# Decoder of two layers on one core: output of the second cross attention added later, two heads rounded at once, sixteen buffers for gathered rows

## Chip, core and metric

The kernel runs on one core of one Trainium2 chip. The metric is the device time of one execution in microseconds; the time before is the median of three runs.

## What is computed

Eight sequences of 256 tokens of width 256 (2048 tokens in all, 16 tiles of 128) go through two decoder layers. Each layer adds to x, one after the other, the results of an attention, a cross attention to a context of 64 tokens and a mixture of experts, each on the layer-normalised x. The part that changes most is the cross attention of the second layer, where the context of all eight sequences counts as one of 512 tokens and queries, keys, values and weights are rounded to whole steps:

```python
q = (x @ Wq + bq).reshape(1, B * N, H, hd)          # 16 heads of 16
kv = (cond @ Wkv + bkv).reshape(1, -1, 2, H, hd)
q, k = _fq_sym(q * scale, axis=-1), _fq_sym(k, axis=-1)
v = _fq_sym(v, axis=2)                               # one step per value column
attn = softmax(einsum('bhqd,bhkd->bhqk', q, k))
attn = _fq_unsigned(attn, axis=-1)                   # round(x / s) * s, s = max / 255
out = einsum('bhqk,bhkd->bhqd', attn, v)
return out @ Wp + bp
# experts of layer 1: 4 of 16 per token, and a shared expert
out = shared / (k + 1) + moe_out * (k / (k + 1))
```

## The kernel before

The five engines run five programs written out ahead, in the order attention, cross attention, experts of layer 0, then the same of layer 1. Each instruction raises a counter, and `at(name, ...)` names the value that another waits for; a queue waits in order, so whatever stands behind a waiting instruction waits with it. SP issues the plain DMAs, POOL (GpSimd) the gathers and scatters by index.

**Second cross attention (class `Cross1`).** The loop runs over 16 steps (h) for each of 16 tiles (t), one score of a head in each step, plus three tiles' worth of steps to drain. Every engine has the same loop with its own lag. In step i PE makes the score of unit i (L1608, one of three PSUM banks, each free after its exponential), the transposes of the rounded weights of unit i-6 (L1618), and every second step the product with the values (L1630). DVE makes the maximum of unit i-1 (L1704) and the rounding of unit i-3 (L1709, five buffers in, five out). POOL makes from the maximum a bias of one column (L1798). ACT makes the exponential of unit i-1 with this bias (L1765) and every second step copies the transposed weights of two heads out of PSUM (L1772). Around these, at fixed h, stand the steps of the tile: the output product of tile t-2 (`pe_o`, h=0) and its addition to x (L1729, h=1), the query product of tile t+1 (`pe_q`, h=2), the seven DVE steps that scale and round the queries (`dve_queries`, one each step from h=3), their build on POOL (L1793, h=9), the transpose (L1602, h=11) and the copy on ACT (L1760, h=12). The output of tile t-1 is normalised at h=9, transposed at h=12 and multiplied at h=13 by the value scales `sv` (L1741, two instructions). POOL adds the output bias to x at h=10 (L1813). In odd tiles DVE and POOL also make the layer norms of two tiles for the experts and two for the next queries (L242 to L257, L250); from the fourth tile on the routing (L1160 to L1194) runs beside the steps, and POOL issues eight scatters to `xs_scratch` (L1381), one every second step from h=14 of an even tile on.

**Experts (class `Experts`).** After the slots of the experts, each token's rows (2 in layer 0, 4 in layer 1) are gathered from `ys_scratch` by POOL (`fetch`, L1406), one DMA for 128 rows, and DVE adds each with its gate to x (`add`, L1326). There are 8 buffers in either layer, and a gather waits for the add that last used its buffer. In layer 1 the shared expert runs in the same stretch for tiles 4 to 15 (products L219, ACT L1371, DVE L1312 and, into x, L1317); DVE's order is two of its steps, then one tile's adds. In layer 0 the adds stand at the head of the attention of layer 1, interleaved with it. SP stores a tile of x after its last add.

## Time and profile before

| | us |
|---|---|
| median of three runs | 1522.99 |
| lowest and highest | 1522.81, 1527.49 |
| profiled execution, its own time | 1528.68 |
| its span | 1526.9 |
| busy: PE, DVE, ACT, POOL | 1214.9, 886.4, 679.5, 429.2 |

The profile is that of one execution. Its rows give the start and the length of an instruction or of several merged, the engine, the line, what is written and read, and in brackets how long the engine had been idle before it and what ended that. Lengths of neighbours overlap a little, since an instruction begins before the one ahead has written all. Starts are counted from the start of the span.

### The profile page before, as it was taken

Reading aid. Unit: us, or ns where it says so; the run is one execution under the profiler, and the core shown is the slowest. Engines: PE = TensorE matmul, PEld = TensorE weight load, DVE = VectorE, ACT = ScalarE, POOL = GpSimd, SP = SyncE. Lnnn points to the kernel's source line nnn. Section 1 sums busy time; section 2 is a strip of 40 time slices with the busy share of each in tenths; the row PEclk is TensorE's granted clock in tenths of the full one; section 3 lists DMA queues with packets and bytes.
Section 4 is the critical chain, followed back from the end, with each engine's and each line's share of the span. In section 5 each row is a group of like instructions: output and inputs, shape, how many; then the busy total and the mean of one; then the engine's idle time right before and its main releaser. Section 6 shows DMA issues by size and latency. Waiting matters only on the chain.

```text
span 1526.9 us, 25789 instructions
## 1 busy us (share of the span) xinstructions
PE 1214.9 (80%) x8208; PEld 848.6 (56%) x8255; DVE 886.4 (58%) x2522; ACT 679.5 (45%) x1412; POOL 429.2 (28%) x682
## 2 busy tenths in 40 slices
PE   5799989982999998478887676777777649999982
PEld 3467766771566665346565354555555435777641
DVE  4546654762232222467676699898888842644354
ACT  2334544320211111134444699989889832333110
POOL 1001101447000000423422243554555441000365
PEclk8799999995999999579898788778787759999997
DMA  7756644012111111543521200000000013454333
GB/s 165 154 118 141 145 107 166 28 42 86 38 44 47 46 45 49 150 103 91 140 58 25 111 2 1 29 22 19 18 29 29 22 49 108 149 155 154 114 103 110
DMA packets 83200, 122.59 MB, mean 80 GB/s; under 512 B 13639, under 2 KB 71111, under 8 KB 79568
## 3 DMA queue, kind: packets, MB, share of 16 engines
q1 hardware_dynamic: 73852, 95.78, 23.5%
q0 software_dynamic: 9216, 25.18, 5.4%
q8 instruction: 69, 1.13, 0.3%
q14 instruction: 63, 0.51, 0.1%
HBM read 76.73 MB, written 43.78 MB: 79 GB/s over the span
## 4 chain that ended last, share of the span: by engine, by line
PE 46%; issue 19%; DVE 11%; POOL 7%; DMA 7%; ACT 6%; SPq 2%; another core or an unknown queue 2%; POOLq 0%; DVEq 0%; ACTq 0%
PE ps L219 13%; PE ps L1070 13%; PE ps L1087 6%; POOL work L1798 3%; DMA W<-q_parts 3%; ACT work L1765 2%; PE ps L423 2%; PE ps L1055 2%; POOL xs_scratch L1381 2%; PE ps L1079 2%; PE ps L443 2%; DVE work L559 1%; PE ps L458 1%; PE ps L426 1%
## 5 line engine op out<-in xcount | busy, mean ns | idle before, releaser
L1070 PE MATMUL ps<-W,work 128*128 x628 | 225.5, 492 | 3.9 <-issue 3.9
L1765 ACT ACTIVATE work<-ps,work 128x512 f32<-128x512 f32 x256 | 204.6, 812 | 31.1 <-POOL work L1798 30.6
L1295 DVE TENSOR_TENSOR work<-work,ps 128x128 f32<-128x128 f32 (+1 forms) x118 | 49.7, 421 | 238.5 <-ACT work L1361 238.5
L1704 DVE TENSOR_REDUCE work<-ps 128x1 f32<-128x512 f32 x256 | 173.3, 677 | 14.3 <-remote 6.9
L559 DVE TENSOR_REDUCE work<-ps 128x2 f32<-128x512 f32 (+1 forms) x192 | 128.3, 685 | 89.8 <-PE ps L426 87.8
L1608 PE MATMUL ps<-SM,work 128*128 128x512 bf16 x209 | 100.9, 485 | 93.4 <-ACT work L1765 91.6
L662 ACT ACTIVATE work<-ps 128x512 f32<-128x512 f32 x192 | 112.9, 601 | 112.8 <-PE ps L446 105.3
L1070 PEld LDWEIGHTS ps<-W,work 128*128 128x128 f32 x628 | 110.9, 191 | 69.0 <-issue 64.7
L1798 POOL TENSOR_SCALAR work<-work 128x1 f32<-128x1 f32 x256 | 93.4, 365 | 176.4 <-DVE work L1704 166.4
L1772 ACT COPY work<-ps 128x1024 bf16<-128x1024 bf16 x128 | 132.1, 1032 | 8.2 <-PE ps L1618 8.1
L250 POOL TENSOR_TENSOR rstd<-ve,half 128x1 f32<-128x1 f32 x96 | 54.3, 571 | 276.7 <-DVE ve L246 274.3
L1618 PE MATMUL ps<-idb,work 128*128 128x128 bf16 x1024 | 122.2, 255 | 6.2 <-ACT work L1765 3.2
L1087 PE MATMUL ps<-W,work 128*128 x470 | 121.0, 380 | 0.0
L1361 ACT ACTIVATE work<-ps 128x128 f32<-128x128 f32 (+1 forms) x118 | 45.4, 384 | 164.2 <-PE ps L1070 164.1
L1406 POOL DMA_INDIRECT W<-ys_scratch,work x64 | 62.8, 982 | 192.6 <-DMA ys_scratch<-work 162.9
L423 PE MATMUL ps<-W 102*128 102x256 bf16 (+3 forms) x512 | 84.3, 273 | 39.1 <-DMA W<-q_parts 19.3
L1709 DVE TENSOR_SCALAR work<-work 128x512 bf16<-128x512 f32 x256 | 108.3, 423 | 11.2 <-ACT work L1765 9.8
L1618 PEld LDWEIGHTS ps<-idb,work 128*128 128x128 bf16 x1024 | 87.6, 115 | 32.5 <-issue 20.7
L1608 PEld LDWEIGHTS ps<-SM,work 128*128 128x128 bf16 x256 | 28.2, 110 | 131.5 <-ACT work L1765 116.6
L219 PE MATMUL ps<-xnT,W 128*128 128x512 f32 (+1 forms) x224 | 90.4, 559 | 6.7 <-ACT work L1371 3.9
L1357 ACT COPY work<-ps 128x256 f32<-128x256 f32 x118 | 44.1, 374 | 97.0 <-PE ps L1055 97.0
L1087 PEld LDWEIGHTS ps<-W,work 128*128 128x128 f32 x470 | 80.2, 190 | 12.1 <-issue 0.4
(246 smaller groups left out, 2366.3 us busy)
## 6 DMA issues: line engine op xcount, KB each, us to landing
work<-xs_scratch SPq DMA_DIRECT2D x118, 128.0 KB, 2.1
ys_scratch<-work SPq DMA_DIRECT2D x118, 128.0 KB, 1.9
q_parts<-work SPq DMA_DIRECT2D x48, 128.0 KB
W<-k_parts SPq DMA_DIRECT2D x48, 128.0 KB
W<-q_parts SPq DMA_DIRECT2D x16, 384.0 KB
W<-in_w_in SPq DMA_DIRECT2D x6, 1024.0 KB, 11.1
W<-q_parts SPq DMA_DIRECT2D x16, 256.0 KB
W<-in_w_out SPq DMA_DIRECT2D x1, 4096.0 KB, 20.0
```

Source lines behind the costliest of these rows:

```text
L219: mm = q.e.matmul(out_, l, r, start=start and i == 0, stop=i == n - 1, skip_group_check=True)
L423: q.e.matmul(PS[bk][:, w * i:w * i + w], qs[0:NA, h, 128 * j:128 * j + 128], ks[0:NA, h // self.per, 0:w], start=i == 0, stop=False, skip_ ...
L559: q.e.tensor_reduce(self.m[:, j, h0:h0 + n], ov, AX, ALU.max).then_inc(*up("mx", L, b, u))
L662: q.e.activation(self.pt(b, g, kind), PS[banks.of["ps2", L, b, g, kind]][:, :], ACT.Exp, scale=0.25).then_inc(*up("exp", L, b, g, kind))
L1070: mm = q.e.matmul(PS[bks[c]][:, 0:N], self.XT[s % 2][:, k, :], w[:, k, bass.ds(regs[s] + 512 * c if c else regs[s], N)], start=k == 0, sto ...
L1087: mm = q.e.matmul(PS[bk][:, 0:256], self.UT[s % 2][:, 128 * c:128 * c + 128], w[:, bass.ds(regs[s] + 256 * c if c else regs[s], 256)], sta ...
L1608: q.e.matmul(PS[bk][:, :], self.q3T[t % 2][:, h // 2, :], kM[:, h, :], start=True, stop=True).then_inc(*up("c1_s", t, h))
L1618: mm = q.e.transpose(PB[bk][:, 512 * (h % 2) + 128 * c:512 * (h % 2) + 128 * c + 128], self.ei[(H * t + h) % 5][:, 128 * c:128 * c + 128], ...
L1704: q.e.tensor_reduce(self.mm[:, h:h + 1], PS[banks.of["c1_s", t, h]][:, :], AX, ALU.max).then_inc(*up("c1_mx", t, h))
L1765: q.e.activation(self.ee[n % 5], PS[banks.of["c1_s", t, h]][:, :], ACT.Exp, bias=self.nb[:, h:h + 1], scale=self.sq[t % 2][:, h:h + 1], ac ...
L1772: q.e.copy(self.aT[n % 3], PB[banks.of["c1_at", n]]).then_inc(*up("c1_aT", n))
L1798: q.e.tensor_scalar(self.nb[:, h:h + 1], self.mm[:, h:h + 1], self.nsq[t % 2][:, h:h + 1], LN255, ALU.mult, ALU.add).then_inc(*up("c1_nb", ...
```

## The change

In the second cross attention, the output is added to x at h=3 instead of h=1, and the queries' steps begin at h=4 instead of 3; their build on POOL moves from h=9 to 10, their transpose from 11 to 12, their copy on ACT from 12 to 13; the output's transpose moves from 12 to 11 and the addition of the output bias from 10 to 11. One instruction rounds the weights of two heads, in even steps, with three buffers of two heads in and two out. The value scales are multiplied into the output weights once, by two instructions at the start of DVE's part, and the transposed output is copied by one instruction. In the experts the adds of a tile wait for all of its gathers, the gathers of a tile for the adds of the tile four before, and layer 1 has 16 buffers.

```diff
-                    self.YG = [xall[1][:, i, :] for i in range(8)]
+                    self.YG = [xall[1][:, i, :] for i in range(16)]
...
             def add(self, q, t):
                 L, K = self.L, self.K
+                q.wait_ge(at(f"g{t % 4}", L, t, K - 1), at("x_b0", t) if L == 0 else at("x_s", t))
                 for j in range(K):
-                    i = (K * t + j) % 8
-                    q.wait_ge(at(f"g{i}", L, t, j), at("x_b0", t) if L == 0 else at("x_s", t), q.chain(), at("x_e", L, t, j - 1))
-                    q.e.scalar_tensor_tensor(out=x[:, t, :], in0=self.YG[i], scalar=self.gk[:, t, j:j + 1], in1=x[:, t, :],
+                    q.wait_ge(q.chain(), at("x_e", L, t, j - 1))
+                    q.e.scalar_tensor_tensor(out=x[:, t, :], in0=self.YG[(K * t + j) % len(self.YG)], scalar=self.gk[:, t, j:j + 1],
...
             def fetch(self, q, t):
+                q.wait_ge(at("x_e", L, t - 4, K - 1))
                 for j in range(K):
-                    i = (K * t + j) % 8
-                    n = K * t + j - 8
-                    q.wait_ge(at("x_e", L, n // K, n % K))
...
-                self.ee = [wk(512) for _ in range(5)]
-                self.ei = [wk(256, BF) for _ in range(5)]
+                self.ee = [wk(1024) for _ in range(3)]
+                self.ei = [wk(512, BF) for _ in range(2)]
...
-                    if h == 11 and t + 1 < T:
+                    if h == 12 and t + 1 < T:
                         self.pe_qt(q, t + 1)
-                    if h == 12 and 1 <= t < T + 1:
+                    if h == 11 and 1 <= t < T + 1:
                         self.pe_ot(q, t - 1)
...
             def dve_round(self, q, t, h):
-                n = H * t + h
-                q.wait_ge(at("c1_exp", t, h), at("c1_at", *self.unit(n - 5)))
-                q.e.tensor_scalar(self.ei[n % 5], self.ee[n % 5], MAGIC, MAGIC, ALU.add, ALU.subtract).then_inc(*up("c1_ei", t, h))
+                n = 8 * t + h // 2
+                q.wait_ge(at("c1_exp", t, h), at("c1_at", *self.unit(2 * n - 3)))
+                q.e.tensor_scalar(self.ei[n % 2], self.ee[n % 3], MAGIC, MAGIC, ALU.add, ALU.subtract).then_inc(*up("c1_ei", n))
...
+                q.wait_ge(at("kv_Vq"), at("w_cr1", "bp"))
+                for k in range(2):
+                    e.tensor_scalar(wp1[:, k, :], wp1[:, k, :], sv[:, k:k + 1], None, ALU.mult).then_inc(*up("c1_wp", k))
...
-                    if 3 <= i < self.N + 3:
+                    if 3 <= i < self.N + 3 and i % 2 == 0:
                         self.dve_round(q, *self.unit(i - 3))
-                    if h == 1 and 2 <= t < T + 2:
+                    if h == 3 and 2 <= t < T + 2:
                         q.wait_ge(at("c1_o", t - 2), at("c1_xb", t - 2))
...
-                    if h == 3 and t + 1 < T:
+                    if h == 4 and t + 1 < T:
                         queries.append(self.dve_queries(q, t + 1))
...
-                        for k in range(2):
-                            m = e.tensor_scalar(self.OnT[:, k, :], PS[banks.of["c1_ot", t - 1]][:, 128 * k:128 * k + 128], sv[:, k:k + 1], None, ALU.mult)
-                            m.then_inc(*(up("c1_OnT", t - 1) if k else q.step()))
+                        e.tensor_copy(self.OnT, halves(PS[banks.of["c1_ot", t - 1]][:, 0:256])).then_inc(*up("c1_OnT", t - 1))
...
-                q.wait_ge(at("c1_nb", t, h), at("c1_ei", *self.unit(n - 5)), at("c1_rs", t - 2))
+                q.wait_ge(at("c1_nb", t, h), at("c1_ei", n // 2 - 3), at("c1_rs", t - 2))
...
-                    if h == 12 and t + 1 < T:
+                    if h == 13 and t + 1 < T:
                         self.act_q3T(q, t + 1)
...
-                    if h == 9 and t + 1 < T:
+                    if h == 10 and t + 1 < T:
                         self.pool_Q3(q, t + 1)
-                    if h == 10 and t < T:
+                    if h == 11 and t < T:
```

## Rows read from the trace of the kernel before

**Rows 1.** Busy time of each engine in the stretch, granted clock, DMA share.
```profile
857.00:1235.00 378.00, 269.02 (x2637) 193.59 (x2681) 331.84 (x918) 340.40 (x675) 182.88 (x361) 0.78 0.06 22
```
**Rows 2.** Groups by form, 857 to 1235: busy us, mean ns, idle before, releasers.
```profile
L1765 ACT ACTIVATE work<-ps,work 128x512 f32<-128x512 f32 x256 | 204.6, 812 | 31.1 <-POOL work L1798 30.6
...
L1704 DVE TENSOR_REDUCE work<-ps 128x1 f32<-128x512 f32 x255 | 172.7, 677 | 10.5 <-PE ps L1608 5.8 <-remote 3.1
L1709 DVE TENSOR_SCALAR work<-work 128x512 bf16<-128x512 f32 x256 | 108.3, 423 | 11.2 <-ACT work L1765 9.8
...
L1729 DVE TENSOR_TENSOR x<-x,ps 128x256 f32<-128x256 f32 x15 | 6.3, 421 | 17.1 <-PE ps L219 17.1
```
**Rows 3.** The exponential's line (L1765): whom it waited for (us, times).
```profile
  POOL work L1798: 30.6, 52
```
**Rows 4.** Tail, POOL: group of the gathers from 1425.7 us, columns as in rows 2.
```profile
L1406 POOL DMA_INDIRECT W<-ys_scratch,work x64 | 62.8, 982 | 192.6 <-DMA ys_scratch<-work 162.9 <-issue 15.2 <-DVE x L1326 14.5
```
**Rows 5.** Tail, POOL in order of time: the first and the last of the 64 gathers.
```profile
1428.74 0.98 POOL L1406 DMA_INDIRECT W<-ys_scratch,work  x1 [162.86 <-DMA ys_scratch<-work]
...
1520.39 0.95 POOL L1406 DMA_INDIRECT W<-ys_scratch,work  x1 [0.30 <-issue]
```
**Rows 6.** Tail, DVE in order of time.
```profile
1451.46 0.42 DVE L1317 SCALAR_TENSOR_TENSOR x<-ps,x 128x256 f32<-128x256 f32 x1 [7.98 <-remote]
...
1505.07 0.42 DVE L1317 SCALAR_TENSOR_TENSOR x<-ps,x 128x256 f32<-128x256 f32 x1 [3.15 <-remote]
1505.41 4.82 DVE L1326 SCALAR_TENSOR_TENSOR x<-W,work,x 128x256 f32<-128x256 f32 x9
...
1523.14 0.48 DVE L1326 SCALAR_TENSOR_TENSOR x<-W,work,x 128x256 f32<-128x256 f32 x1 [0.61 <-DMA W<-ys_scratch,work]
```
**Rows 7.** Order of time, start of an even tile.
```profile
1038.44 2.02 PE L219 MATMUL ps<-W,work 128*128 128x256 f32 x4
...
1040.25 0.63 PE L1608 MATMUL ps<-SM,work 128*128 128x512 bf16 x1
...
1040.50 0.42 DVE L1729 TENSOR_TENSOR x<-x,ps 128x256 f32<-128x256 f32 x1 [1.43 <-PE ps L219]
...
1040.83 0.25 DVE L1160 MAX8 work<-ctxN 128x8 f32<-128x16 f32 x2
...
1041.20 0.69 DVE L1704 TENSOR_REDUCE work<-ps 128x1 f32<-128x512 f32 x1
...
1044.07 0.38 PE L1608 MATMUL ps<-SM,work 128*128 128x512 bf16 x1
...
1044.48 0.68 DVE L1704 TENSOR_REDUCE work<-ps 128x1 f32<-128x512 f32 x1
```
**Rows 8.** Order of time, DVE: rounding of 1024 elements while the values are prepared.
```profile
830.23 0.69 DVE L1513 TENSOR_SCALAR W<-W 128x1024 bf16<-128x1024 f32 x1
```
**Rows 9.** Order of time, a bias in step 5 of the odd tile.
```profile
1022.29 0.26 POOL L1798 TENSOR_SCALAR work<-work 128x1 f32<-128x1 f32 x1
```
**Rows 10.** Order of time, steps 12 and 13 of an odd tile.
```profile
1033.12 1.06 POOL L1381 DMA_INDIRECT xs_scratch<-W,work  x1
...
1033.71 1.02 ACT L1760 COPY work<-ps 128x1024 bf16<-128x1024 bf16 x1
...
1034.12 0.41 DVE L1709 TENSOR_SCALAR work<-work 128x512 bf16<-128x512 f32 x1
1034.27 0.39 POOL L1798 TENSOR_SCALAR work<-work 128x1 f32<-128x1 f32 x1
...
1034.70 0.78 ACT L1765 ACTIVATE work<-ps,work 128x512 f32<-128x512 f32 x1
...
1035.47 1.00 ACT L1772 COPY work<-ps 128x1024 bf16<-128x1024 bf16 x1
...
1036.36 0.79 ACT L1765 ACTIVATE work<-ps,work 128x512 f32<-128x512 f32 x1
```
**Rows 11.** Layer 0, DVE: last add of the second tile.
```profile
617.87 0.48 DVE L1326 SCALAR_TENSOR_TENSOR x<-SM,ctxN,x 128x256 f32<-128x256 f32 x1 [0.18 <-DMA SM<-ys_scratch,ctxN]
```

More of the change, by code:

```diff
@@ L1322, in add @@
                 L, K = self.L, self.K
+                q.wait_ge(at(f"g{t % 4}", L, t, K - 1), at("x_b0", t) if L == 0 else at("x_s", t))
                 for j in range(K):
-                    i = (K * t + j) % 8
-                    q.wait_ge(at(f"g{i}", L, t, j), at("x_b0", t) if L == 0 else at("x_s", t), q.chain(), at("x_e", L, t, j - 1))
-                    q.e.scalar_tensor_tensor(out=x[:, t, :], in0=self.YG[i], scalar=self.gk[:, t, j:j + 1], in1=x[:, t, :],
-                                             op0=ALU.mult, op1=ALU.add).then_inc(*up("x_e", L, t, j))
+                    q.wait_ge(q.chain(), at("x_e", L, t, j - 1))
+                    q.e.scalar_tensor_tensor(out=x[:, t, :], in0=self.YG[(K * t + j) % len(self.YG)], scalar=self.gk[:, t, j:j + 1],
+                                             in1=x[:, t, :], op0=ALU.mult, op1=ALU.add).then_inc(*up("x_e", L, t, j))
             def vector(self, q):
@@ L1401, in fetch @@
                 q.wait_ge(*y_stored(L), at("sc", L, T - 1, K - 1), at("idy", L), at("x_b0", T - 1) if L == 0 else None)
+                q.wait_ge(at("x_e", L, t - 4, K - 1))
                 for j in range(K):
-                    i = (K * t + j) % 8
-                    n = K * t + j - 8
-                    q.wait_ge(at("x_e", L, n // K, n % K))
-                    q.e.indirect_dma_start(self.YG[i], None, YS[0:128 * self.NT, :], bass.IndirectOffsetOnAxis(ap=self.idy[:, t, j:j + 1], axis=0)).then_inc(
-                        *landing(f"g{i}", L, t, j))
+                    q.e.indirect_dma_start(self.YG[(K * t + j) % len(self.YG)], None, YS[0:128 * self.NT, :],
+                                           bass.IndirectOffsetOnAxis(ap=self.idy[:, t, j:j + 1], axis=0)).then_inc(*landing(f"g{t % 4}", L, t, j))
             def sync(self, q):
@@ L1615, in pe_turn @@
                 bk = banks.of["c1_at", n]
-                q.wait_ge(at("c1_ei", t, h))
+                q.wait_ge(at("c1_ei", n))
                 for c in range(4):
                     mm = q.e.transpose(PB[bk][:, 512 * (h % 2) + 128 * c:512 * (h % 2) + 128 * c + 128],
-                                       self.ei[(H * t + h) % 5][:, 128 * c:128 * c + 128], idb[:, :])
+                                       self.ei[n % 2][:, 512 * (h % 2) + 128 * c:512 * (h % 2) + 128 * c + 128], idb[:, :])
                 mm.then_inc(*up("c1_at", t, h))
@@ L1642, in pe_o @@
                 bk, free = banks.take(self.r1, ("c1_o", t), [("x_c1", t)])
-                q.wait_ge(at("c1_OnT", t), *free)
+                q.wait_ge(at("c1_OnT", t), at("c1_wp", 1), *free)
                 pair_mms(q, PS[bk][:, 0:256], [(self.OnT[:, k, :], wp1[:, k, :]) for k in range(2)]).then_inc(*up("c1_o", t))
@@ L1763, in act_exp @@
                 n = H * t + h
-                q.wait_ge(at("c1_nb", t, h), at("c1_ei", *self.unit(n - 5)), at("c1_rs", t - 2))
-                q.e.activation(self.ee[n % 5], PS[banks.of["c1_s", t, h]][:, :], ACT.Exp, bias=self.nb[:, h:h + 1],
+                q.wait_ge(at("c1_nb", t, h), at("c1_ei", n // 2 - 3), at("c1_rs", t - 2))
+                q.e.activation(self.ee[n // 2 % 3][:, 512 * (h % 2):512 * (h % 2) + 512], PS[banks.of["c1_s", t, h]][:, :], ACT.Exp, bias=self.nb[:, h:h + 1],
                                scale=self.sq[t % 2][:, h:h + 1], accum_out=self.se[t % 2][:, h:h + 1]).then_inc(*up("c1_exp", t, h))
```

## Prediction

> **What bounds the kernel now.** I read the busy time by stretch first, then the waits of the second cross attention, then the order of time at its tile borders, then the tail. The stage from 857 to 1235 us has two nearly full engines: ACT is busy 340.4 of 378 us and DVE 331.8 [rows 1]. So what DVE saves is worth something only where ACT sits idle for want of DVE's work. ACT's exponentials sit idle 31.1 us in all, 30.6 of them in 52 waits until POOL's one-column bias (called the bias here) is there, and DVE's largest wait is 17.1 us for the output product before it adds it to x [rows 2, 3]. The tail, from 1428.7 us on, is POOL's 64 gathers. They take 1.255 us each when nothing is in the way (0.95 busy and 0.30 between), 62.8 us busy in all, and in between POOL waits 14.5 us for DVE's adds, because a gather needs one of 8 buffers back [rows 4, 5]. The last add starts at 1523.14 us [rows 6], and with the last store the span ends at 1526.9.
>
> In what follows h is the step of the 16-step loop of a tile, and a step's score is the one of head h.
>
> **Output added at h=3 instead of 1.** This removes DVE's wait, up to 17.1 us. Is it on the path? At the start of an even tile PE spends 2.02 us from 1038.44 on the output product, then starts the score of head 1 at 1040.25 and has it at about 1040.88; DVE's add starts at 1040.50 and its maximum of head 1 at 1041.20 [rows 7]. With the add gone the maximum must still wait for that score, which is behind the same product in PE's queue. The gain there is at most 0.3 us, and the 0.33 us of the add (until DVE's next, at 1040.83) comes back two steps later. The next border is the same: the score of head 3 starts at 1044.07 behind the query product, and the maximum at 1044.48 follows it at once [rows 7]. So the wait goes, and a wait for the score is late next. I take 0. The bounds are 17.1 us of gain (if DVE alone bound it) and 1 us of loss, since in odd tiles the add now stands beside the normalisation statistics in step 3. Queries move from h=3 to 4: their one wait, part of the same border, goes the same way, 0.
>
> **Two heads rounded at once.** 256 instructions of 0.423 us become 128 of 1024 elements [rows 2]. The trace has such a one on the same kind of operand: 0.69 us [rows 8]. Against 0.846 for two this saves 0.16 us of duration; taking off the 0.09 by which neighbours on DVE overlap (the add of 1040.50 takes 0.42 and its neighbour starts 0.33 later [rows 7]), 0.07. So 9 to 20 us less of DVE over the stage, but even steps get 0.27 us longer and odd ones 0.33 shorter. Where ACT runs without a gap (most of the stage) it buys nothing; the border is PE's. I take 0, with both bounds kept: 20 us of gain, and the loss below. The two buffers mean that a rounding waits for the transposes one PE step back rather than two; these stand right behind the score that DVE's maximum needs, and that maximum itself takes 0.68 [rows 2], so 0. The three double buffers of exponentials hold as many heads as before, 0.
>
> **The loss in the same edit.** The bias of 1022.29, with no rounding beside it, takes 0.26 us [rows 9]. The one at 1034.27 runs beside a rounding that began at 1034.12 and took 0.41, and it takes 0.39, ending 0.13 after it [rows 10]. A rounding that takes 0.69 would hold it to 0.28 us later than now, in even steps.
> The Trainium skill, SBUF — State Buffer, section SBUF: two separate sides, says why: DVE's two-port modes, which a float32 tensor_scalar in SBUF can enter, take a port pair shared with GpSimd for the whole instruction. The trace agrees; that rule speaks against this change and would make the sum that of the third rival.
>
> **Copy of the queries on ACT from h=12 to 13, its build on POOL from 9 to 10, bias add of x from 10 to 11.** In the odd tiles 5 to 13 POOL issues scatters. At h=12 it makes a bias, a reciprocal root, a scatter of 1.06 us at 1033.12, and only then the next bias at 1034.27, for the exponential at 1034.70 [rows 10]. ACT is free at 1033.71 and fills the gap with the query copy, which holds it for 0.89 us (as the copy of 1035.47 does until 1036.36) [rows 10]. After the change the copy comes behind that exponential, so ACT idles from 1033.71 to 1034.70 and then does the 0.89 us. Everything behind it, the scores of the next tile too, is late by that. On POOL the build now stands ahead of the scatter of step 10 and the bias add ahead of step 12's bias; with the held bias this is 0 to 0.4 us, I take 0.2. Cost: 5 tiles x 1.1 = **+5.5 us**. Bounds: 0 (if other things are late there anyway, as a rearranged DVE may make them) and 1.3 x 6 = 8. In even tiles, without scatters, ACT has no gap at this step: 0.
> The swapped transposes (queries at 12, output at 11) are the same work on PE, beside ACT's: 0.
>
> **Value scales in the output weights.** 16 times two DVE instructions of the output transpose become one, some 3 us of DVE, counted with the rounding at 0. New are two of 128x256 at the start, nothing beside them. The nearest row is the rounding, twice as wide, at 0.423 [rows 2]: half of it each (none to the whole as bounds), **+0.4 us**.
>
> **Adds wait for the whole tile.** In layer 0 the second tile's last add started at 617.87, on its own gather, with its first done [rows 11]. Now both of a tile wait for the last, so one add of 0.48 us is added behind it, in a stretch in which all wait: **+0.5 us**. The fetch of layer 0 now waits for a tile's last add rather than each its own: under 0.6 us, hidden behind attention.
>
> **Sixteen buffers.** Unhindered, 64 gathers would be issued by 1428.74 + 64 x 1.255 = 1509.1 us instead of 1521.3 [rows 5]. But the gathers of tile 15 wait for the adds of tile 11, and those wait behind DVE's last output of the shared experts, at 1505.07; the nine adds from 1505.41 take 4.82 us, so four end at 1507.6 [rows 6]. Tile 15 then: start 1508.0, last gather 3 x 1.255 later, landing 2.75 us after its issue (from the 1520.39 gather to the 1523.14 add [rows 5, 6]), and four adds (the first three now come after the last landing, 0.55 each): last add starts at 1508.0 + 3.8 + 2.75 + 1.65 = 1516.2. DVE's own 20 adds from 1505.4 give about 1516.0. Against 1523.14: **-6.9 us**. Nothing of PE's part moves: its shared experts end where they do now. The out stores follow the adds as before.
>
> **Sum.** 5.5 + 0.4 + 0.5 - 6.9 = -0.5 us. The profiled execution took 1528.68 us (span 1526.9, 1.8 around it), 0.4% above the median 1522.99; the change applied to it gives 1528.2, to the median **1522.5 us**. A measurement of this kernel tells 0.3% (4.6 us) from no change.
>
> **Rivals.**
> 1. *ACT's gaps close with DVE's relief.* For it: DVE's waits of 17.1 us and the reduction in instructions; the gaps before exponentials sum to 31.1. If a third of these go (10 us) and the copy's gap (5.5) doesn't open: 1522.5 - 15.5 = 1507. Against it: the border, where the score sets the pace [rows 7]. 0.24.
> 2. *Only the copy's gap stays closed*, because the rearranged DVE and POOL are late elsewhere in the odd tile and the copy fits there: 1522.5 - 5.5 = 1517. 0.14.
> 3. *The wider rounding holds the bias.* In its place, even steps in which ACT waits for the bias: about 26 of the 52 waits [rows 3], 0.28 each, 7 us; it decides once the hold costs more than the 0.07 us that a pair saves on DVE. 1530. Against: waits behind POOL's own scatters are among them, such as the one for the bias of 1034.27 [rows 10]. 0.10.
> 4. *The tail gives nothing.* DVE waits 7.98 us before 1451.46, without a releaser that the trace can name [rows 6]. If a burst of gathers causes it, longer bursts make longer waits, and what POOL gains DVE loses: 1522.5 + 6.9 = 1529.5. The same time comes if the new buffers don't do what they say, the fetch still waiting on adds. 0.18. Were the wait to vanish instead, the last shared output would come up to 8 us before 1505.07 and the gathers alone would bound it (1507.8 + 2.75 + 1.65 = 1512.2 for the last add): 1518.5, the edge of the forecast's own range.
>
> **Numbers.** Forecast (no change, 1518.5 to 1527.5) 0.34. Faster: rivals 1 and 2, 0.38. Slower: 3 and 4, 0.28. The range takes in rivals 1 and 4 and the bound of 8 us on the copy: 1507 to 1532.
>
> **What would show it.** The DVE add without a wait, but as many maxima waiting for scores; a gap of about 1 us on ACT ahead of the exponential before the query copy in five odd tiles; biases of even steps that end 0.8 us after the rounding starts; two tiles 1 us longer than now; gathers in one row with hardly a wait for adds, and the last add 7 us nearer to 1505. I am wrong if the stage from first to last exponential shrinks by more than 3 us, or if the last shared output comes later than now relative to the first gather.

## The result, and the profile after

The changed kernel takes 1537.6 us (median of 20 runs, 1524.8 to 1545.5) against 1523.0 for the kernel before beside it (20 runs, 1518.8 to 1530.2). The ratio is 1.0086, 95% interval 1.0067 to 1.0105: **13 us slower** (0.86% of 1523), above the forecast range of 1507 to 1532. The profiled execution of after took 1535.01 us (span 1533.2), 2.5 under its median; that of before 1528.68, 5.7 over its own. So the two traces differ by 6.3 us of the 13, and sums are made against the ratio.

*The attention.* Its first exponential starts at 855.8 us (857.1 before) and its last at 1236.2 (1229.6), so the stage grew from 372.6 to 380.4 us: 7.9. Busy time in the same stretch as [rows 1]:

```profile
857.00:1235.00 378.00, 264.61 (x2572) 185.29 (x2616) 316.97 (x759) 337.57 (x665) 201.29 (x358) 0.77 0.06 20
```

DVE is busy 15 us less, as forecast, and POOL 18 us more. The groups by form of that stretch (busy us, mean ns, idle before them, releasers) answer to [rows 2]:

```profile
L1765 ACT ACTIVATE work<-ps,work 128x512 f32<-128x512 f32 x254 | 201.6, 805 | 34.8 <-POOL work L1798 33.0
L1702 DVE TENSOR_REDUCE work<-ps 128x1 f32<-128x512 f32 x253 | 170.8, 678 | 29.5 <-PE ps L1606 22.2 <-remote 6.5 <-POOL work L1798 0.4
...
L1798 POOL TENSOR_SCALAR work<-work 128x1 f32<-128x1 f32 x253 | 109.7, 434 | 160.0 <-DVE work L1702 143.6 <-ACT work L1765 8.0
...
L1708 DVE TENSOR_SCALAR work<-work 128x1024 bf16<-128x1024 f32 x127 | 89.9, 708 | 21.4 <-ACT work L1765 20.6
...
L1731 DVE TENSOR_TENSOR x<-x,ps 128x256 f32<-128x256 f32 x14 | 5.7, 409 | 0.0
```

The add's wait of 17.1 us is gone, and the maxima's wait for scores rose from 5.8 to 22.2: one for the other. What is new is the bias (L1798): 434 ns in the mean instead of 365. In order of time, one bias in step 2 of an odd tile, and the exponential that waits for it:

```profile
1069.17 0.68 DVE L1708 TENSOR_SCALAR work<-work 128x1024 bf16<-128x1024 f32 x1
1069.35 0.63 POOL L1798 TENSOR_SCALAR work<-work 128x1 f32<-128x1 f32 x1 [0.87 <-DVE work L1702]
1070.02 0.78 ACT L1765 ACTIVATE work<-ps,work 128x512 f32<-128x512 f32 x1 [0.38 <-POOL work L1798]
```

The one-column operation takes 0.63 us and ends 0.13 us after the rounding. And steps 12 and 13 of the same tile, as [rows 10]:

```profile
1083.79 1.06 POOL L1381 DMA_INDIRECT xs_scratch<-W,work  x1 [0.20 <-issue]
1084.93 0.26 POOL L1798 TENSOR_SCALAR work<-work 128x1 f32<-128x1 f32 x1
1085.23 0.78 ACT L1765 ACTIVATE work<-ps,work 128x512 f32<-128x512 f32 x1 [1.38 <-POOL work L1798]
...
1086.00 1.00 ACT L1772 COPY work<-ps 128x1024 bf16<-128x1024 bf16 x1
1086.89 1.02 ACT L1760 COPY work<-ps 128x1024 bf16<-128x1024 bf16 x1
1087.80 0.80 ACT L1765 ACTIVATE work<-ps,work 128x512 f32<-128x512 f32 x1
```

The gap is open (1.38 us) and the query copy of 1086.89 holds ACT 0.91 us behind it, step for step as worked out.

*The tail.* From the last exponential to the first gather nothing changed (199.1 and 198.7 us). The gathers, as [rows 4, 5]:

```profile
L1404 POOL DMA_INDIRECT W<-ys_scratch,work x64 | 61.8, 966 | 193.4 <-DMA ys_scratch<-work 163.2 <-issue 17.7 <-DVE x L1326 12.6
```
```profile
1434.90 0.98 POOL L1404 DMA_INDIRECT W<-ys_scratch,work  x1 [163.15 <-DMA ys_scratch<-work]
...
1526.09 0.95 POOL L1404 DMA_INDIRECT W<-ys_scratch,work  x1 [0.30 <-issue]
```

POOL still waits 12.6 us for adds (14.5 before), with twice the buffers. DVE in order of time, as [rows 6], and PE beside its first wait:

```profile
1450.56 0.42 DVE L1317 SCALAR_TENSOR_TENSOR x<-ps,x 128x256 f32<-128x256 f32 x1 [2.04 <-PE ps L219]
1463.23 0.42 DVE L1317 SCALAR_TENSOR_TENSOR x<-ps,x 128x256 f32<-128x256 f32 x1 [12.24 <-remote]
...
1474.48 0.76 DVE L1317 SCALAR_TENSOR_TENSOR x<-ps,x 128x256 f32<-128x256 f32 x2 [8.88 <-remote]
...
1517.06 0.42 DVE L1317 SCALAR_TENSOR_TENSOR x<-ps,x 128x256 f32<-128x256 f32 x1 [0.65 <-issue]
1517.40 5.97 DVE L1326 SCALAR_TENSOR_TENSOR x<-W,work,x 128x256 f32<-128x256 f32 x12
...
1529.01 2.05 DVE L1326 SCALAR_TENSOR_TENSOR x<-W,work,x 128x256 f32<-128x256 f32 x4 [3.00 <-DMA W<-ys_scratch,work]
```
```profile
1446.43 7.17 PE L219 MATMUL ps<-W,work 128*128 128x256 f32 x32 [0.85 <-issue]
1453.44 5.31 PE L219 MATMUL ps<-xnT,W 128*128 128x512 f32 x12
```

PE's rows have the four shared outputs (32 products) done by 1453.6, the second of them by about 1450.0, but DVE goes on with the second only at 1463.23. The 12.24 us stand where before had 7.98. The last shared output comes 82.2 us behind the first gather (76.3 before) and the last add 95.7 (94.4): what is gained behind the shared experts is lost ahead of them. This is one of the two signs that the prediction named for being wrong.

### The profile page after: what moved, and what is told of

Same layout as the page of the kernel before. It is cut to its first block, busy times and chain, and to the rows that moved or that the text cites. A ratio compares the mean times of both kernels' runs of the same rounds, so it can differ in the third digit from the quotient of the medians.

```text
span 1533.2 us, 25353 instructions
## 1 busy us (share of the span) xinstructions
PE 1210.2 (79%) x8208; PEld 841.3 (55%) x8255; DVE 876.3 (57%) x2380; ACT 683.2 (45%) x1412; POOL 446.3 (29%) x682
## 4 chain that ended last, share of the span: by engine, by line
PE 44%; issue 19%; POOL 11%; DVE 8%; DMA 7%; ACT 5%; another core or an unknown queue 3%; SPq 3%; POOLq 0%; DVEq 0%; ACTq 0%
PE ps L1070 13%; PE ps L219 12%; PE ps L1087 6%; POOL work L1798 5%; DMA W<-q_parts 3%; POOL xs_scratch L1381 3%; ACT work L1765 2%; PE ps L423 2%; DVE work L559 2%; PE ps L1055 2%; PE ps L1079 2%; PE ps L443 2%; POOL rstd L250 1%; PE ps L458 1%
## 5 line engine op out<-in xcount | busy, mean ns | idle before, releaser
L1765 ACT ACTIVATE work<-ps,work 128x512 f32<-128x512 f32 x256 | 203.2, 805 | 36.6 <-POOL work L1798 34.7
L1702 DVE TENSOR_REDUCE work<-ps 128x1 f32<-128x512 f32 x256 | 172.7, 678 | 33.2 <-PE ps L1606 22.2
L1798 POOL TENSOR_SCALAR work<-work 128x1 f32<-128x1 f32 x256 | 110.5, 432 | 164.3 <-DVE work L1702 147.9
L423 PE MATMUL ps<-W 102*128 102x256 bf16 (+3 forms) x512 | 82.4, 268 | 40.8 <-DMA W<-q_parts 20.8
L1606 PEld LDWEIGHTS ps<-SM,work 128*128 128x128 bf16 x256 | 27.5, 108 | 140.4 <-ACT work L1765 113.2
L1708 DVE TENSOR_SCALAR work<-work 128x1024 bf16<-128x1024 f32 x128 | 90.6, 708 | 22.4 <-ACT work L1765 20.6
L1087 PEld LDWEIGHTS ps<-W,work 128*128 128x128 f32 x470 | 80.4, 191 | 12.2 <-issue 0.5
```

The costliest lines, as they stand in the source:

```text
L423: q.e.matmul(PS[bk][:, w * i:w * i + w], qs[0:NA, h, 128 * j:128 * j + 128], ks[0:NA, h // self.per, 0:w], start=i == 0, stop=False, skip_ ...
L1087: mm = q.e.matmul(PS[bk][:, 0:256], self.UT[s % 2][:, 128 * c:128 * c + 128], w[:, bass.ds(regs[s] + 256 * c if c else regs[s], 256)], sta ...
L1606: q.e.matmul(PS[bk][:, :], self.q3T[t % 2][:, h // 2, :], kM[:, h, :], start=True, stop=True).then_inc(*up("c1_s", t, h))
L1702: q.e.tensor_reduce(self.mm[:, h:h + 1], PS[banks.of["c1_s", t, h]][:, :], AX, ALU.max).then_inc(*up("c1_mx", t, h))
L1765: q.e.activation(self.ee[n // 2 % 3][:, 512 * (h % 2):512 * (h % 2) + 512], PS[banks.of["c1_s", t, h]][:, :], ACT.Exp, bias=self.nb[:, h:h ...
L1798: q.e.tensor_scalar(self.nb[:, h:h + 1], self.mm[:, h:h + 1], self.nsq[t % 2][:, h:h + 1], LN255, ALU.mult, ALU.add).then_inc(*up("c1_nb", ...
```

## Experiments

The kernels ran in five groups, each on one chip and beside the kernel before: chips A to E, on which before has medians of 1524.4, 1514.9, 1524.7, 1523.4 and 1513.5 us. All ratios are to before on the same chip. Two tables hold what was measured; ratios are of medians, the rest is from the trace of one execution each. The attention's goes by the starts of the exponentials: the stage from first to last, and the mean length of even (4 to 12) and odd (5 to 13) tiles. Eleven traces of kernels that have the attention of before show stages of 368.3 to 375.4 us, even tiles of 23.4 to 23.7 and odd ones of 24.1 to 24.3, so smaller differences than these spreads mean nothing.

| attention | chip | ratio, 95% interval | stage us | even | odd | bias ns |
|---|---|---|---|---|---|---|
| before | | 1 | 372.6 | 23.60 | 24.31 | 365 |
| after | | 1.0086, 1.0067 to 1.0105 | 380.4 | 23.15 | 26.04 | 434 |
| x_only | A | 1.0062, 1.0035 to 1.0089 | 380.6 | 23.19 | 26.22 | 432 |
| x_unmoved | A | 1.0100, 1.0076 to 1.0123 | 386.9 | 23.95 | 26.09 | 422 |
| copy13 | A | 1.0057, 1.0035 to 1.0080 | 382.0 | 23.63 | 25.63 | 362 |
| x_copyback | B | 1.0056, 1.0032 to 1.0080 | 384.7 | 23.69 | 25.92 | 430 |
| x_narrow | B | 1.0036, 1.0015 to 1.0058 | 375.8 | 22.87 | 25.35 | 361 |
| narrow_copyback | B | 1.0006, 0.9989 to 1.0024 | 370.5 | 22.89 | 24.43 | 362 |
| wide_only | B | 1.0055, 1.0027 to 1.0083 | 380.4 | 24.14 | 25.32 | 427 |
| even_late | D | 0.9997, 0.9975 to 1.0019 | 372.2 | 23.07 | 25.03 | 360 |

| tail | chip | ratio, 95% interval | last shared output | last add | unnamed waits, ACT + DVE us | all idle, ACT + DVE us |
|---|---|---|---|---|---|---|
| before | | 1 | 76.3 | 94.4 | 32.6 + 20.8 | 59.7 + 27.6 |
| after | | 1.0086 | 82.2 | 95.7 | 49.5 + 21.1 | 71.4 + 31.5 |
| x_only | A | 1.0062 | 77.0 | 95.1 | 32.7 + 24.1 | 59.8 + 28.8 |
| x_unmoved | A | 1.0100 | 72.5 | 92.7 | 0 + 15.1 | 55.0 + 23.7 |
| copy13 | A | 1.0057 | 76.8 | 94.9 | 19.4 + 16.0 | 59.0 + 29.4 |
| g_only | A | 1.0027, 1.0003 to 1.0050 | 90.0 | 100.9 | 46.5 + 35.6 | 70.9 + 42.5 |
| the four on chip B | B | | 62.3 | 82.6 to 82.7 | 0 + 0 | 51.1 + 5.0 to 5.5 |
| before_again | C | 1.0014, 0.9987 to 1.0041 | 73.8 | 93.2 | 25.5 + 8.6 | 62.4 + 14.2 |
| g_only_2 | C | 1.0020, 0.9995 to 1.0046 | 79.9 | 95.4 | 34.1 + 22.5 | 69.7 + 27.7 |
| no_gather | C | 0.9873, 0.9835 to 0.9911 | | | 0 + 0 | 51.1 + 6.5 |
| plain_rows | C | 0.9890, 0.9857 to 0.9923 | | | 0 + 0 | 51.1 + 6.5 |
| land_wait | D | 1.0094, 1.0059 to 1.0130 | 76.0 | 109.8 | 0 + 0 | 59.6 + 1.1 |
| pause | D | 1.0009, 0.9984 to 1.0035 | 73.9 | 95.4 | 24.4 + 3.1 | 59.1 + 12.6 |
| even_late | D | 0.9997 | 76.6 | 94.7 | 32.6 + 18.7 | 58.9 + 29.1 |
| g_only_3 | D | 1.0038, 1.0018 to 1.0058 | 90.4 | 101.3 | 46.8 + 38.4 | 70.6 + 43.4 |
| pause8 | E | 1.0036, 1.0007 to 1.0065 | 62.3 | 87.3 | 0 + 0 | 51.1 + 5.4 |
| pause8_sixteen | E | 1.0009, 0.9985 to 1.0034 | 62.4 | 88.0 | 0 + 0 | 51.1 + 3.5 |

In the tail's table the times count from the first gather. An unnamed wait is one whose releaser the trace gives as "remote", before ACT's activation (L1371) or DVE's shared output (L1317); "all idle" is everything that the two engines waited before these twelve instructions each. An unnamed wait is not all delay: on chip B ACT waits 10.9 us for PE at the head of the second and of the third block of four tiles, and such a wait is counted whole where its releaser has no name. What the tail loses is better read from the last shared output.

### The change cut in two

x_only is after with the tail's three hunks taken back, g_only is before with those three alone:

```
-                    self.YG = [xall[1][:, i, :] for i in range(8)]
+                    self.YG = [xall[1][:, i, :] for i in range(16)]
...
+                q.wait_ge(at(f"g{t % 4}", L, t, K - 1), at("x_b0", t) if L == 0 else at("x_s", t))
...
+                q.wait_ge(at("x_e", L, t - 4, K - 1))
```

> Every part of the change in the second cross attention, and the gathers and adds as they were before. Theory A (my sum was right for the attention and wrong for the tail): the stage from first to last exponential is 5 to 8 us longer than the 372.5 us of before (after has 380.4), and the tail from the first gather to the last add is that of before, so the kernel is 5 to 9 us slower than before, and some 5 to 8 us faster than the change whole. Theory B (the whole loss is in the attention, the tail's stalls come from when it starts and not from the gathers): as slow as the change whole, about 13 us over before. Theory C (the loss is all in the tail): within 3 us of before.

> The kernel before with only the sixteen buffers and the waits by whole tile in fetch and add. Theory A (the prediction's fourth rival: longer bursts of gathers make longer waits without a named releaser on DVE and ACT, so that the last shared output comes 5 to 8 us later relative to the first gather): 0 to 7 us slower than before. My forecast's sum for this part, if the attention's change is what disturbed the tail: 6 us faster, last add about 87 us behind the first gather instead of 94.8. Theory C (it alone carries the loss): 13 us slower.

The attention costs 9.5 us (0.62% of 1524), the tail 4.1, together 13.6 where 13.1 are to be explained; each is known to some 4 us. Theory A holds for both halves, with the attention's 9.5 us just above its 5 to 9. In g_only the last shared output comes 13 us later than in x_only, though, and not 5 to 8.

### The attention's parts

x_unmoved is x_only with six steps put back; queries and output's add both stand at 3:

```
-                    if h == 4 and t + 1 < T:
+                    if h == 3 and t + 1 < T:
                         queries.append(self.dve_queries(q, t + 1))
...
-                    if h == 13 and t + 1 < T:
+                    if h == 12 and t + 1 < T:
                         self.act_q3T(q, t + 1)
```

> As the run with the attention's parts alone, but the steps of the queries, their build and copy, the bias add and the two transposes are put back where they were; the output's add stays at step 3, the rounding stays at two heads, the value scales stay in the output weights. Theory A (the copy of the queries behind the exponential of step 13 costs 0.9 to 1.1 us in five tiles): 4.5 to 6 us faster than with the moves, so 0 to 3 us over before. Rival (the held biases of the wide rounding are the cost: 7 us): as slow as with the moves, and the biases' mean stays at about 0.43 us. Second rival (DVE's relief pays once the moves are gone): faster than before by up to 10 us.

A miss: slower than with the moves, by 6 us. Step 12 of odd tiles is indeed back at 1.66 us (2.57 with the moves), but step 3 went from 2.21 to 2.79 and the first four steps of even tiles from 6.95 to 7.98. That spoke for a cost of the rounding itself, larger where queries stand beside it.

copy13 is before with the last hunk the other way, 12 to 13:

> The kernel before with one number changed: ACT copies the queries of the next tile at step 13 instead of 12. Theory A: in the five odd tiles 5 to 13 ACT idles about 1 us ahead of the exponential of step 13 and does the 0.89 us of the copy behind it, so the stage is 4.5 to 5.5 us longer and the kernel 4 to 6 us slower. Rival (the gap is filled or the time comes back at the tile border, where PE sets the pace): within 1 us of before.

8.7 us slower, above theory A's 4 to 6 (the interval begins at 5.3). Step 12 of odd tiles is 0.90 us longer (1.66 to 2.56), as forecast; step 15 and the next step 0 together 0.85 more (0.83 to 1.30, 2.77 to 3.15), which was not. PE and DVE of copy13 in order of time, odd tile, step 14, then PE of before, and then of x_narrow (below), which has the late copy and the swapped transposes:

```profile
1084.15 1.89 PE L219 MATMUL ps<-W,xnT 128*128 128x16 f32 x8 [1.11 <-ACT work L1760]
1085.88 0.59 PE L1608 MATMUL ps<-SM,work 128*128 128x512 bf16 x1
1086.50 0.69 DVE L1704 TENSOR_REDUCE work<-ps 128x1 f32<-128x512 f32 x1 [1.17 <-PE ps L1608]
```
```profile
1083.87 1.51 PE L219 MATMUL ps<-W,xnT 128*128 128x16 f32 x8
1085.22 0.59 PE L1608 MATMUL ps<-SM,work 128*128 128x512 bf16 x1
```
```profile
1084.21 1.65 PE L219 MATMUL ps<-W,xnT 128*128 128x16 f32 x8
```

The transposes and the router's product take two PSUM banks in turn. In copy13 the product gets the bank that the late copy (L1760) reads, waits 1.11 us in PE's queue, and the next score is 0.66 later. The change itself swaps PE's transposes too, so that the product gets the other bank; in x_narrow it starts at 1084.21, ahead of the late copy at 1084.50, and step 15 stays at 0.83. The swap, which I costed at 0, thus keeps a wait away. How much it is worth was not run by itself: a late copy makes a pair of tiles 1.35 us longer without the swap (copy13) and 0.90 with it (x_narrow against narrow_copyback); these are 0.45 apart, no more than the spread of such sums.

Four kernels on chip B cross the two suspects. x_copyback is x_only with copy, build, transposes and bias add back, x_narrow is x_only with single rounding, narrow_copyback both, wide_only before with the rounding of two and nothing else:

```
-                    if 3 <= i < self.N + 3:
+                    if 3 <= i < self.N + 3 and i % 2 == 0:
                         self.dve_round(q, *self.unit(i - 3))
```

> The attention's parts of the change, with the query copy on ACT back at step 12, its build at 9, its transposes at 11 (the output's at 12) and the bias add at 10; unlike the run with all moves undone, the queries of DVE stay at step 4. Theory A (the copy behind the exponential costs 0.9 us in each odd tile; what slowed the run with all moves undone was queries and output's add both at step 3, between the scatters of the odd tiles): 6 to 9 us faster than the run with the attention's parts, so within 2 us of before; the stage from first to last exponential takes 371 to 375 us. Rival (moving the copy back brings the slow steps 2 and 3 back, whatever the queries do): as slow as the run with all moves undone, 387 us for the stage.

> The attention's parts of the change, but each head rounded by itself again with five buffers. Theory A (the rounding of two costs 0.27 us wherever the exponential waits for a bias that it holds, my third rival): 5 to 9 us faster than the attention's parts with it, stage 372 to 376 us, mean bias back at about 0.37 us. Rival (the rounding of two earns its relief and the copy's place is the only cost): as slow or slower by up to 5 us, stage 381 to 386.

> Both of the above at once: before, with the output's add at step 3, the queries at 4, and the value scales in the output weights. Theory A (both costs are taken away and the tile border keeps the 0.7 us per even tile that it won in the changed kernel): 3 to 8 us faster than before, stage 365 to 370 us. Rival (that border gain came from the rounding of two, the border being DVE's only with it): within 2 us of before, stage 371 to 374.

> The kernel before with two heads rounded at once and nothing else. Theory A (held biases): biases at even steps end 0.27 us later, 7 to 14 us slower than before. Rival (a saving of 0.07 to 0.16 us a pair on a full DVE): up to 10 us faster. My own sum for this part: 0.

With neither: +0.06%. The moves alone: +0.36%, so 4.6 us for them. The rounding: +0.56% and, by itself in before, +0.55%, so 7.6 to 8.3 us. Both: +0.62% (x_only, chip A). The two together seem to cost less than their sum; the intervals, 3 to 4 us each way, don't settle that, but the tile means do: over narrow_copyback a pair of tiles is 0.90 us longer with the moves, 2.29 with the rounding and 2.09 with both. That a late bias and a late copy are paid for with the same time is my reading and was not shown. x_copyback missed its theory (371 to 375 expected, 384.7 found). x_narrow met it in stage and bias, and is faster than x_only by 0.26% or 4 us where 5 to 9 were expected, on two chips. narrow_copyback missed its theory in time and has its rival's (within 2 us), but even tiles keep the border's 0.7 us (22.89), so the rival's reason, that this gain came from the rounding, is not the right one. wide_only met its theory. At the start of its even tile 10, in order of time:

```profile
1098.54 0.68 DVE L1709 TENSOR_SCALAR work<-work 128x1024 bf16<-128x1024 f32 x1
1098.72 0.64 POOL L1798 TENSOR_SCALAR work<-work 128x1 f32<-128x1 f32 x1 [2.89 <-DVE work L1704]
1099.39 0.78 ACT L1765 ACTIVATE work<-ps,work 128x512 f32<-128x512 f32 x1 [0.29 <-POOL work L1798]
```

The same bias takes 0.37 us in before (at 1089.78 us), and there ACT doesn't wait for it; here it waits 0.29 us. The hold is larger behind a scatter. Step 3 of odd tile 9, POOL, DVE and ACT of wide_only, then POOL and ACT of before:

```profile
1077.40 0.84 POOL L1798 TENSOR_SCALAR work<-work 128x1 f32<-128x1 f32 x1
1077.49 0.68 DVE L1709 TENSOR_SCALAR work<-work 128x1024 bf16<-128x1024 f32 x1
1078.28 0.78 ACT L1765 ACTIVATE work<-ps,work 128x512 f32<-128x512 f32 x1 [1.92 <-POOL work L1798]
```
```profile
1070.07 0.26 POOL L1798 TENSOR_SCALAR work<-work 128x1 f32<-128x1 f32 x1
1070.37 0.78 ACT L1765 ACTIVATE work<-ps,work 128x512 f32<-128x512 f32 x1 [1.34 <-POOL work L1798]
```

In before no rounding runs beside this bias; now one does, and bias and wait grow by 0.58 us each, and so they do in the mean of the five odd tiles. Over the stage the exponentials' waits for biases grow from 30.6 to 36.3 us, 5.7 of the 7.9 by which wide_only's stage is longer. The Trainium skill, SBUF — State Buffer, section SBUF: two separate sides, has the rule (DVE's two-port modes keep a port pair from GpSimd for the whole instruction), and the trace agrees in the length of the hold. The bias of 1077.40 is recorded as starting 0.08 us ahead of the rounding and is held all the same.

even_late asks whether the late add's gain can be had alone:

```
-                    if h == 1 and 2 <= t < T + 2:
+                    if h == (1 if t % 2 else 3) and 2 <= t < T + 2:
...
-                    if h == 3 and t + 1 < T:
+                    if h == (3 if t % 2 else 4) and t + 1 < T:
```

> The kernel before with the output's add at step 3 and the queries at step 4 in even tiles only, where the run with both moves and narrow rounding won 0.7 us at each border; odd tiles as before. Theory A (that gain is the border's own): 3 to 6 us faster than before, stage from first to last exponential 366 to 369 us. Rival (what the border gives comes back in the odd tile behind it): within 2 us.

It went the rival's way: even tiles give 0.53 us, odd ones take back 0.72. No kernel faster than before came of it.

### The tail's waits

The four kernels on chip B had no unnamed wait and a tail of 82.7 us. ACT's and DVE's groups of narrow_copyback (chip B) from 1425 us on, then ACT's of before in the same stretch:

```profile
L1371 ACT ACTIVATE work<-ps 128x512 f32<-128x512 f32 x11 | 6.6, 599 | 47.2 <-PE ps L219 47.2
...
L1317 DVE SCALAR_TENSOR_TENSOR x<-ps,x 128x256 f32<-128x256 f32 x12 | 5.1, 423 | 5.5 <-PE ps L219 5.5
```
```profile
L1371 ACT ACTIVATE work<-ps 128x512 f32<-128x512 f32 x12 | 7.1, 599 | 59.7 <-remote 32.6 <-DVE work L1312 14.1 <-PE ps L219 13.0
```

So on chip C the unchanged kernel was profiled too. Of the others one leaves the gathers out, and one puts plain transfers of neighbouring rows in their place:

```
                 else:
-                    for t in range(T):
-                        self.fetch(q, t)
...
+                    q.e.dma_start(self.YG[i], YS[128 * (K * t + j):128 * (K * t + j) + 128, :]).then_inc(*landing(f"pg{t % 2}", L, t, j))
```

> The kernel before, unchanged, for a profile on the chip of the other runs of this call. The four runs of the last call all had a tail of 82.7 us from the first gather to the last add, without one of the long waits that no releaser is named for, where the five of the first call had 92.7 to 99.4. Theory P (those waits belong to the chip that it runs on, not to the kernel): this run shows either no such wait and 82.7 us, or some of 4 to 8 us each and 92 to 96 us, and the others of this call show the same kind. Rival Q (the attention's edits of the last call shifted the tail's phase and so cured it): 94 us here, whatever the chip.

> Before with only the sixteen buffers and the waits by tile, a second time. If the chip is one without the long waits: the gathers came every 1.27 us with eight buffers already (63 x 1.27 = 79.9 us from first to last), so the new buffers can give nothing; three more adds behind the last landing and one in the first cross attention's stretch give 1 to 2 us slower, last add 84 to 85 us behind the first gather. If it is one with them: 0 to 8 us slower, last add 95 to 101. My forecast's sum, 6 us faster, would need a last add at 87 on the one or 76 on the other.

> Before with the 64 gathers of layer 1 left out (the adds read whatever the buffers hold). Theory A (the gathers' traffic makes the waits without a releaser): no such wait is left on DVE or ACT, the last shared output comes about 62 us behind the first shared product of block 1 as in the stall-free runs, or sooner, and the last add follows within 6 us. Rival (the waits have another cause, such as the fetch of instructions): on a chip that has them they stay, 5 to 12 us each.

> Before with the 64 gathers of layer 1 replaced by plain transfers of SP, of the same size and into the same buffers but of 128 neighbouring rows (the values are not the right ones), issued two tiles ahead. If it is POOL's software-made transfers that hold the other engines, the long waits vanish on a chip that has them; if it is the traffic of 1 KB rows, they stay. On a chip without them it tells what bounds the tail: with POOL's 0.95 us an issue gone, the last shared output comes sooner than 62 us and the last add within 70 us of the first transfer if the gathers set the pace, and at 82 if PE and DVE do.

(The tails on chip A reach to 100.9, in g_only, and not to 99.4 as the first of these expectations has it.) On a chip where before_again has unnamed waits (a DVE one of 7.09 us, an ACT one of 17.30), neither kernel without POOL's gathers has one, though plain_rows moves the same bytes. The group of ACT from 1425 us on in no_gather; that of plain_rows reads the same:

```profile
L1371 ACT ACTIVATE work<-ps 128x512 f32<-128x512 f32 x12 | 7.2, 598 | 51.1 <-PE ps L219 51.1
```

In before the same twelve waits sum to 59.7 us and DVE's to 27.6, against 51.1 and 6.5 here.

Theory P holds as far as it was seen: chips A, C and D show the waits, B and E don't, and the median of before is 9 to 11 us lower on the latter, close to the tail's 94.4 less 82.7. The kernel before itself was not profiled on B or E: on B the four kernels share its tail, on E both pause, and only the median says that before had no waits there either.

Then the length of a row of gathers. land_wait makes POOL wait for a tile's landings before the next tile's gathers; pause puts one addition of 128x256 behind each tile's, pause8 behind every second's, pause8_sixteen the same with sixteen buffers:

```
                     for t in range(T):
+                        if t:
+                            q.wait_ge(*[at(f"g{(K * t - 1 - j) % 8}", L, t - 1, K - 1 - j) for j in range(K)])
                         self.fetch(q, t)
```
```
                         self.fetch(q, t)
+                        q.wait_ge(q.chain())
+                        q.e.tensor_tensor(self.XB[0], self.XB[0], bp1, ALU.add).then_inc(*q.step())
```

> The kernel before, but POOL waits for the landing of a tile's four gathers before it issues those of the next, so no row of gathers is longer than four (before: up to 24 in a row; with sixteen buffers: 33). Theory A (on the chips that show them, the waits without a releaser on DVE and ACT last while POOL issues gathers and end when it pauses): none is over 3 us here; the gathers themselves take 16 x (5.0 + about 1.5) = 104 us, so the last add comes about 106 us behind the first gather and the kernel is 10 to 14 us slower. Rival (their length has nothing to do with rows of gathers): some of 5 to 12 us stay. On a chip without them: only the 106 us show.

> The kernel before, with one addition of 128x256 on POOL (0.72 us by its like in the trace) behind each tile's gathers. Theory A (a short pause in POOL's gathers lets the delayed signals through): on a chip with the long waits they shrink to under 3 us, and the tail comes to 80 + 16 x 1.0 = 96 us by POOL's own work, or to what DVE needs: 0 to 4 us slower than before, but the last shared output 8 to 14 us sooner relative to the first gather (62 to 66 us). Rival (0.72 us of other work on POOL is no pause that matters): the last shared output stays at 74 to 76 us. On a chip without them: 12 to 16 us slower, shared output at 62.

> Before with only the sixteen buffers and the waits by tile, a third time, for the chip of this call. With the long waits (two chips so far): 2 to 6 us slower than before (the two calls gave 4.1 and 3.0), last add 94 to 101 us behind the first gather. Without them (one chip so far): 1 to 2 us slower, last add at 84 to 85, gathers in one row of 64 at 1.27 us as with eight buffers.

On chip D: rows of four gathers with a wait for their landing leave no unnamed wait, rows broken by 0.8 us of an addition leave 27.5 us of them, sixteen buffers 85.2, and even_late, whose tail is that of before, 51.3. But neither way of keeping rows short gives time. land_wait is 14 us slower and its last shared output comes at 76.0, no sooner than even_late's 76.6. pause missed its theory: one wait is still 16.2 us, and the last shared output comes at 73.9, which is the rival's 74 to 76 and not 62 to 66. g_only_3, DVE, then POOL in order of time:

```profile
1444.12 0.42 DVE L1317 SCALAR_TENSOR_TENSOR x<-ps,x 128x256 f32<-128x256 f32 x1 [8.63 <-remote]
...
1460.27 0.42 DVE L1317 SCALAR_TENSOR_TENSOR x<-ps,x 128x256 f32<-128x256 f32 x1 [13.76 <-remote]
```
```profile
1463.69 0.95 POOL L1404 DMA_INDIRECT W<-ys_scratch,work  x1 [7.37 <-DVE x L1326]
```

POOL ran through its sixteen buffers while DVE waited 13.76 us, and then waited 7.37 us for adds itself. pause is no faster than before (1.0009).

> As the run with one POOL addition behind each tile's gathers, but behind every second tile only, so that rows of eight gathers stay and POOL's own work is 80 + 8 x 0.9 = 87 us. Theory A (rows of 18 to 24 make waits of 7 to 8 us, rows of four with a short pause at most 3.6): waits without a releaser up to about 5 us, 30 to 45 us of them on ACT and DVE together (before 53, with a pause for each tile 27.5), last add 90 to 93 us behind the first gather, kernel 1 to 4 us faster than before. Rival (what the pause saves in waits it costs on POOL): within 1 us, as with the pause for each tile. On the chip without long waits: 5 to 7 us slower, last add at 90.

> The sixteen buffers and waits by tile, with the same POOL addition behind every second tile. Theory A (the sixteen buffers cost because they let rows of 33 gathers through, and the rows are what counts): with rows of eight they cost no more than the three extra adds at the end, within 2 us of the run with eight buffers and the pause. Rival (a short pause does not end a row, POOL's waits for adds do): 3 to 6 us slower than that run, waits of 8 to 14 us. On the chip without long waits: equal to that run within 2 us, both with the last add at 90 to 91.

Chip E has no such waits, so neither tells of rows of eight on a chip that does. They tell of the buffers where nothing is late and both kernels pause: 88.0 us to the last add against 87.3, and ratios 0.27% apart in favour of sixteen, with overlapping intervals. Whether sixteen buffers give a little there stays open; that they cost is not seen. A break every eight gathers costs 5 us (82.7 to 87.3).

Sixteen buffers and the waits by tile always ran together, so the runs don't part them.

## Why the prediction was wrong

- **Output added late: 0.** Right (narrow_copyback, +0.06%). Its wait of 17.1 us became the maxima's 22.2 us for scores. The cost of standing beside other work in odd tiles shows most where queries stand at 3 too (x_unmoved).
- **Rounding of two: 0, in its place +7.6 to 8.3.** This step failed: the hold of the bias was worked out and then left out of the sum. It stood in the prediction as its third rival, with 0.28 us a bias (0.27 measured at an even tile's start) and 7 us in all, and was given 0.10 because other waits were POOL's own scatters. The scatters do not shield it. A bias behind a scatter, which ran alone before, now runs beside a rounding and is held by 0.58: in wide_only step 3 of odd tiles went from 2.21 to 2.79 us. Step 9 went from 1.56 to 2.01, and the border's step 0 from 2.77 to 3.43, of which the 0.29 above are a part. The relief of 15 us on DVE bought nothing; the forecast had said so.
- **Query copy: +5.5, measured 4.6** (x_narrow against narrow_copyback, known to some 3 us). Right, with step 12 longer by 0.91 where 0.89 was forecast. What was left out is the bank: the copy alone costs 8.7 (5.3 to 12.2), and the swapped transposes, costed at nothing, may win part of the difference back.
- **Added up.** Rounding and moves give 9.5 in x_only, where the two measured alone sum to 12.2 to 12.9; the tile means say that they overlap, the times leave it open.
- **Value scales and layer 0: +0.9.** Not separated; narrow_copyback, which has the scales, is within 0.06%. In layer 0 the second tile's pair of adds starts at 619.86 after and its last add at about 620.4, against 617.87 [rows 11], of which 1.5 us come from gathers that start later: about 1 us, forecast 0.5, from one trace each.
- **Sixteen buffers: -6.9, in its place +4.3** (with the waits by tile: 4.1, 3.0 and 5.8 us). This is the other step that failed. Behind the last shared output the last add does come sooner (13.5 us instead of 18.1), but the last shared output itself moved by 5.8. The clause "Nothing of PE's part moves: its shared experts end where they do now" is the wrong one: on chips A and D the last shared output comes 13 us or more later with sixteen buffers, on C 6. The fourth rival said how and had 0.18. It priced the tail at no gain, 6.9 over the forecast; the measured cost lies 10.7 over the forecast's tail with its 0.5 for layer 0. Nor was the forecast's gain seen on a chip without late waits.
- **The two rivals were alternatives in the sum and both came.** Rival 3 and rival 4 are in different stages; the forecast plus both is 1522.5 + 7 + 6.9 = 1536.4, near the 1537.6 measured. The range took in each, never the two. That their sum comes so near is partly luck: the tail cost more than its rival said, and rounding and moves less than their sum.

## What to carry to other kernels

Rivals that live in different stages add, so the range must hold their sum. A wider DVE instruction saves DVE time, but as measured here it holds the small GpSimd operations beside it until it ends, and that counts wherever their reader is already waiting. Before moving a step on one engine, look up who takes the bank it frees. In a tail with long unnamed waits, don't count on what unhindered issue would give.

## What the runs showed of the hardware

- On chips A, C and D, as in the first profiles, ACT and DVE wait long and without a named releaser for PE's products while POOL issues gathers in a row; on B and E they don't (tail 94 against 82.7 us, whole kernel 9 to 11 us). On C the waits are gone without POOL's gathers and with plain transfers of the same size.
- With sixteen buffers rows of up to 28 gathers come instead of 20 (the expectations' counts of 24 and 33 were too high), and the last shared output is later on the same chip: 90.0 against 72.5 to 77.0 us on A (three kernels with eight buffers), 79.9 against 73.8 on C, 90.4 against 76.6 on D. The unnamed waits go the same way but vary more: on A 15.1, 35.4 and 56.7 us with eight buffers, 82.1 with sixteen. That it is the length of the rows that does it was not shown, since the two kernels with rows of four have their last shared output at 76.0 and 73.9.
- Why the products' signals come late, and why some chips don't show it, stays open; whether the products themselves are late can't be told, as their ends are modelled.
- Without those waits, gathers were issued every 1.27 us (63 in 79.9 us) with eight buffers, and the last add follows the last gather by 2.8 us: they set the end of the kernel.
- A one-column GpSimd operation took 0.26 us with no DVE rounding beside it, 0.37 beside one of 512 columns, and 0.63 to 0.84 beside one of 1024, ending 0.07 to 0.13 us after it.
